# Loading and splitting q and k of the first pair of heads in the stage before the attention

## The reference

```python
qkv = xm @ W_qkv
q, k, v = jnp.split(qkv, 3, axis=-1)          # each (4, 1024, 1024), reshaped to 16 heads of 64
attn = jnp.einsum('bqhd,bkhd->bhqk', q, k) * 64 ** (-0.5)
attn = jax.nn.softmax(attn, axis=-1)
out = jnp.einsum('bhqk,bkhd->bqhd', attn, v).reshape(4, 1024, 1024)
x = x + g_msa * (out @ W_out + b_out)
```

## Time and profile before

| what | value |
|---|---|
| median of 3 runs | 3242.78 us (3240.78 to 3244.02) |
| the profiled execution | 3242.52 us |
| its span in the trace | 3240.4 us |
| projections, first product to last | 557.5 to 1106.4 us |
| attention, first scores to last product with v | 1121.3 to 2274.7 us |
| PE busy | 95% of the span |
| DVE busy | 59% |
| ACT busy | 39% |
| POOL busy | 27% |

### The profile page before, as it was taken

How to read it: one execution, slowest core, us unless ns; L and a number is a source line. 1 busy time by engine, 2 the same in 40 slices (tenths; PEclk the granted TensorE clock), 3 DMA queues, 4 the chain that set the end, 5 groups by cost and what they waited for, 6 DMA issues and landing times. The chain is left out here.

```text
span 3240.4 us, 61734 instructions
## 1 busy us (share of the span) xinstructions
PE 3084.6 (95%) x24696; PEld 2441.5 (75%) x24696; DVE 1904.3 (59%) x2802; ACT 1250.9 (39%) x2370; POOL 863.8 (27%) x578
## 2 busy tenths in 40 slices
PE   8969996999999799999999999999896999999999
PEld 5968885888888677777777777777685888888887
DVE  4369996111221288888888888888564333343332
ACT  2123332222222177777777777777002111111111
POOL 1012222100000044354445434446454111111110
PEclk9989998999999899999999999999997999999999
DMA  4543322333333433323333333332563001000100
GB/s 139 181 181 129 102 72 90 104 106 105 100 104 110 114 99 90 99 80 93 94 92 86 87 104 82 87 93 80 207 237 121 1 27 32 26 32 26 33 14 14
DMA packets 196387, 297.25 MB, mean 92 GB/s; under 512 B 27937, under 2 KB 105761, under 8 KB 194103
## 3 DMA queue, kind: packets, MB, share of 16 engines
q1 hardware_dynamic: 182576, 276.54, 27.4%
q0 software_dynamic: 4288, 14.68, 1.3%
q10 hardware_dynamic: 9296, 2.77, 0.4%
HBM read 190.44 MB, written 103.49 MB: 91 GB/s over the span
## 5 line engine op out<-in xcount | busy, mean ns | idle before, releaser
L1267 DVE TENSOR_REDUCE b_nm<-b_ps 128x1 f32<-128x1024 f32 x512 | 601.9, 1217 | 16.3 <-PE b_ps L1208 3.2
L1174 ACT ACTIVATE b_p<-b_ps,b_nm 128x1024 f32<-128x1024 f32 x512 | 565.0, 1113 | 41.2 <-DVE b_nm L1267 41.2
L1237 PE MATMUL b_po<-b_pt,b_v 128*64 128x256 f32 x4096 | 498.3, 385 | 0.8 <-DVE b_pt L1287 0.8
L1179 ACT ACTIVATE b_pt<-b_tp_act 128x512 f32<-128x512 f32 x512 | 308.7, 603 | 304.9 <-PE b_tp_dve L1220 304.9
L1287 DVE COPY b_pt<-b_tp_dve 128x512 f32<-128x512 f32 x512 | 351.5, 686 | 116.9 <-PE b_tp_dve L1220 116.8
L1220 PEld LDWEIGHTS b_tp_act<-ident,b_p 64*128 64x128 f32 x4096 | 312.1, 138 | 129.4 <-issue 100.6
L1237 PEld LDWEIGHTS b_po<-b_pt,b_v 128*64 128x64 f32 x4096 | 271.8, 136 | 128.7 <-ACT b_pt L1179 0.9
L1220 PE MATMUL b_tp_act<-ident,b_p 64*128 64x64 f32 x4096 | 347.7, 225 | 2.4 <-issue 2.4
L1220 PE MATMUL b_tp_dve<-ident,b_p 64*128 64x64 f32 x4096 | 347.5, 225 | 0.0
L1629 ACT ACTIVATE d_ge<-d_pf,d_b 128x512 f32<-128x512 f32 x128 | 88.1, 689 | 598.6 <-PE d_pf L1651 598.6
L1718 DVE CAST d_gh<-d_ge 128x512 fp32r<-128x512 f32 x128 | 68.7, 537 | 421.5 <-ACT d_ge L1629 421.5
(11 more groups left out here) (228 smaller groups left out, 5771.3 us busy)
## 6 DMA issues: line engine op xcount, KB each, us to landing
b_raw_q<-q_t SPq DMA_DIRECT2D x128, 256.0 KB, 4.4
q_t<-p_qk SPq DMA_DIRECT2D x64, 256.0 KB, 2.0
k_t<-p_qk SPq DMA_DIRECT2D x64, 256.0 KB, 2.0
v_n<-p_vs SPq DMA_DIRECT2D x32, 512.0 KB, 3.2
b_raw_k<-k_t SPq DMA_DIRECT2D x128, 128.0 KB, 4.4
b_v<-v_n SPq DMA_DIRECT2D x32, 512.0 KB, 3.9
b_rb<-inv SPq DMA_DIRECT2D x64, 256.0 KB, 3.8
o_t<-b_ot SPq DMA_DIRECT2D x32, 512.0 KB, 2.6
```

The costliest lines, as they stand in the source:

```text
L1174: act.activation(pr[k % 4][:], ps[k % 2][:], ACT.Exp, bias=nm[:, k % 4:k % 4 + 1], accum_out=rs[:, n:n + 1]).then_inc(exp_done, 1)
L1179: act.activation(dst, src, ACT.Copy).then_inc(t_out[0], 1)
L1237: mm = pe.matmul(po[rows, (blk % 2) * 2 * P:(blk % 2 + 1) * 2 * P], vt[u][:, kc, rows], pt[blk % 2][h][:, kc, :], start=(kc == 0), stop=(k ...
L1267: dve.tensor_reduce(nm[:, k % 4:k % 4 + 1], ps[k % 2][:], axis=AX.X, op=ALU.max, negate=True).then_inc(max_done, 1)
```

## The change

`program` now allocates eight tiles, `pair0` (the halves of q and k for the two heads of pair 0), before `projections` and on the right side of SBUF, and frees them after `attention`. In the last group of `projections` SP issues the eight loads of pair 0 ahead of the group's first store, into raw tiles of that stage. `q_t[0]` and `k_t[0]` were written in groups 0 and 1. DVE waits for all eight loads and makes the eight split operations ahead of the copies of v. In `attention` set 0 of the halves is `pair0`. The eight first loads, the eight split operations, the waits on `first_split` in PE and POOL and three semaphores are gone. `projections` has two semaphores more.

```diff
@@ -739,7 +739,7 @@
     dve.tensor_scalar(var_eps[:], mean_var[:, :, 1], EPS, None, ALU.add).then_inc(var_ready, 1)
 
 
-def projections(nc, t, ident, mod_t, y, q_t, k_t, v_n, wqk):
+def projections(nc, t, ident, mod_t, y, q_t, k_t, v_n, pair0, wqk):
 
 
 
@@ -764,6 +764,8 @@
         xl = ring(ctx, nc, "p_xl", 2, [P, KC, 512], F32R)
         qk = ring(ctx, nc, "p_qk", 4, [P, 512], F32)
         vs = ring(ctx, nc, "p_vs", 2, [P, INNER], F32)
+        raw_q = ring(ctx, nc, "p_raw_q", 2, [P, S], F32)
+        raw_k = ring(ctx, nc, "p_raw_k", 2, [P, S // 2], F32)
         pt = banks(ctx, nc, "p_pt", 2)
         pm = banks(ctx, nc, "p_pm", 4)
         (w_split, ln_step, half_set, var_ready, rstd_ready, z_done, t_done, xm_done, rounded, x_split,
@@ -771,6 +773,7 @@
             ctx, nc, "proj", "w_split ln_step half_set var_ready rstd_ready z_done t_done xm_done rounded x_split mb_done "
             "m_done qk_done v_done w_rounded qk_free v_free", first=True)
         w_in, ones_set = sems(ctx, nc, "proj", "w_in ones_set")
+        pair_in, pair_rounded = sems(ctx, nc, "proj", "pair_in pair_rounded")
         first_in = sems(ctx, nc, "proj", " ".join("first_in%d" % i for i in range(GT)))
         y_in = sems(ctx, nc, "proj", "y_in0 y_in1")
         qk_out = sems(ctx, nc, "proj", " ".join("qk_out%d" % i for i in range(4)))
@@ -800,9 +803,19 @@
             sp.sem_inc(qk_free, 4)
             sp.sem_inc(v_free, 2)
 
+            def load_pair0():
+                for h in range(2):
+                    for half in range(2):
+                        rows = slice(half * D1, (half + 1) * D1)
+                        sp.dma_start(raw_q[h][rows, :], q_t[0, h * D1:(h + 1) * D1, :]).then_inc(pair_in, 16)
+                        sp.dma_start(raw_k[h][rows, :], k_t[0, h * D1:(h + 1) * D1, half * S // 2:(half + 1) * S // 2]
+                                     ).then_inc(pair_in, 16)
+
             def turn(b, last):
                 for hf in range(2):
                     g = b * 2 + hf
+                    if last and hf:
+                        load_pair0()
                     for n in range(NQK):
                         dst = q_t if n < PAIRS else k_t
                         sp.wait_ge(qk_done, g * NQK + n + 1)
@@ -975,6 +988,14 @@
                         norm(g + 1, b + hf, 1 - hf)
                         normed(g + 1, 1 - hf, 0)
                         normed(g + 1, 1 - hf, 1)
+                    if not more:
+                        dve.wait_ge(pair_in, 128)
+                        for h in range(2):
+                            dve.tensor_copy(pair0["qh"][h][:], raw_q[h][:])
+                            dve.tensor_copy(pair0["kh"][h][:], raw_k[h][:]).then_inc(pair_rounded, 1)
+                            dve.wait_ge(pair_rounded, h + 1)
+                            dve.tensor_tensor(pair0["ql"][h][:], raw_q[h][:], pair0["qh"][h][:], ALU.subtract)
+                            dve.tensor_tensor(pair0["kl"][h][:], raw_k[h][:], pair0["kh"][h][:], ALU.subtract)
                     for m in range(NV):
                         n = m // 2
                         if more and m % 2 == 0:
@@ -987,7 +1008,7 @@
             turn(B - 1, True)
 
 
-def attention(nc, t, ident, q_t, k_t, v_n, inv, o_t, wo, wo_raw, o_first, o_first_raw):
+def attention(nc, t, ident, q_t, k_t, v_n, pair0, inv, o_t, wo, wo_raw, o_first, o_first_raw):
 
 
 
@@ -1015,10 +1036,10 @@
             return ctx.enter_context(nc.sbuf_tensor("b_" + name, shape, dt))
         raw_q = ring(ctx, nc, "b_raw_q", 2, [P, S], F32)
         raw_k = ring(ctx, nc, "b_raw_k", 2, [P, SK], F32)
-        qh = [ring(ctx, nc, f"b_qh{u}", 2, [P, S], F32R) for u in range(2)]
-        ql = [ring(ctx, nc, f"b_ql{u}", 2, [P, S], F32R) for u in range(2)]
-        kh = [ring(ctx, nc, f"b_kh{u}", 2, [P, SK], F32R) for u in range(2)]
-        kl = [ring(ctx, nc, f"b_kl{u}", 2, [P, SK], F32R) for u in range(2)]
+        qh = [pair0["qh"], ring(ctx, nc, "b_qh", 2, [P, S], F32R)]
+        ql = [pair0["ql"], ring(ctx, nc, "b_ql", 2, [P, S], F32R)]
+        kh = [pair0["kh"], ring(ctx, nc, "b_kh", 2, [P, SK], F32R)]
+        kl = [pair0["kl"], ring(ctx, nc, "b_kl", 2, [P, SK], F32R)]
         vt = ring(ctx, nc, "b_v", 2, [P, BT, P], F32)
         pr = ring(ctx, nc, "b_p", 4, [P, S], F32)
         pt = [ring(ctx, nc, f"b_pt{u}", 2, [P, BT, 2 * P], F32) for u in range(2)]
@@ -1032,13 +1053,12 @@
         tp_dve = banks(ctx, nc, "b_tp_dve", 2)
         po, = banks(ctx, nc, "b_po", 1)
         (q_in, ones_set, raw_used, rounded, qk_ready, s_done, max_done, exp_done, inv_done, inv_turned, inv_stored, rb_in,
-         t_done, av_done, o_out, o_scaled, o_stored, o_free, first_split, ri_clear) = sems(
+         t_done, av_done, o_out, o_scaled, o_stored, o_free, ri_clear) = sems(
             ctx, nc, "attn", "q_in ones_set raw_used rounded qk_ready s_done max_done exp_done inv_done inv_turned inv_stored rb_in "
-            "t_done av_done o_out o_scaled o_stored o_free first_split ri_clear", first=True)
+            "t_done av_done o_out o_scaled o_stored o_free ri_clear", first=True)
         t_out = sems(ctx, nc, "attn", "t_out0 t_out1")
         t_begun, = sems(ctx, nc, "attn", "t_begun")
         wo_in, next_rounded, next_split, o_first_in = sems(ctx, nc, "attn", "wo_in next_rounded next_split o_first_in")
-        first_in = sems(ctx, nc, "attn", "first_in0 first_in1")
         v_in = sems(ctx, nc, "attn", "v_in0 v_in1")
         block = ctx.enter_context(nc.Block())
 
@@ -1060,11 +1080,6 @@
                              ).then_inc(v_in[u], 16)
 
             def first_load():
-                for h in range(2):
-                    for half in range(2):
-                        sp.dma_start(raw_q[h][HALF[half], :], q_t[0, HALF[h], :]).then_inc(first_in[h], 16)
-                        sp.dma_start(raw_k[h][HALF[half], :], k_t[0, HALF[h], half * SK:(half + 1) * SK]
-                                     ).then_inc(first_in[h], 16)
                 sp.dma_start(vt[0][:], v_n[0].rearrange("(c k) d -> k c d", k=P)).then_inc(v_in[0], 16)
 
             def spread(p, u):
@@ -1132,7 +1147,6 @@
                 pool.wait_ge(rb_in, 32 * p + 32)
                 pool.tensor_tensor(ot[u][:], ot[u][:], rb[u][:], ALU.mult).then_inc(o_scaled, 1)
 
-            pool.wait_ge(first_split, 4)
             pool.sem_inc(raw_used, 1)
             split(1, 0, 1)
             with pool.Fori(0, LAST2) as i:
@@ -1197,9 +1211,7 @@
                 g, u, s = i * TS + k, (k // STEPS) % 2, k % STEPS
                 h = (s // 2) % 2
                 q0 = (s // QB) * 2 * P + (s % 2) * P
-                if k in (0, 2):
-                    pe.wait_ge(first_split, k + 2)
-                elif s == 0:
+                if k and s == 0:
                     pe.wait_ge(qk_ready, i * TURN + k // STEPS)
                 if k >= 2:
                     pe.wait_ge(exp_done, g - 1)
@@ -1302,13 +1314,6 @@
             dve.memset(ri[:], 0.0).then_inc(ri_clear, 1)
             dve.wait_ge(ri_clear, 1)
 
-            for h in range(2):
-                dve.wait_ge(first_in[h], 64)
-                dve.tensor_copy(qh[0][h][:], raw_q[h][:])
-                dve.tensor_copy(kh[0][h][:], raw_k[h][:]).then_inc(first_split, 1)
-                dve.wait_ge(first_split, 2 * h + 1)
-                dve.tensor_tensor(ql[0][h][:], raw_q[h][:], qh[0][h][:], ALU.subtract)
-                dve.tensor_tensor(kl[0][h][:], raw_k[h][:], kh[0][h][:], ALU.subtract).then_inc(first_split, 1)
             maximum(0, 0)
             maximum(1, 1)
             for k in range(0, TS, 2):
@@ -1800,14 +1805,18 @@
             raw, rest = over_raw(part, nc, name, shape)
             return (high, rest), raw
 
+        first_pair = ExitStack()
         with ExitStack() as part:
             wqk, wqk_raw = split_pair(part, "w_qk", [P, KC, 2 * INNER])
             graph_attention(nc, t, ident, gp, cg, pn, y, wqk, wqk_raw)
-            projections(nc, t, ident, mod_t, y, q_t, k_t, v_n, wqk)
+            pair0 = {name: [first_pair.enter_context(nc.sbuf_tensor(f"pair0_{name}{h}", [P, cols], F32R, side="right"))
+                            for h in range(2)] for name, cols in (("qh", S), ("ql", S), ("kh", S // 2), ("kl", S // 2))}
+            projections(nc, t, ident, mod_t, y, q_t, k_t, v_n, pair0, wqk)
         with ExitStack() as part:
             wo, wo_raw = split_pair(part, "w_out", [P, INNER // P, F])
             o_first, o_first_raw = split_pair(part, "o_first", [P, INNER // P, 512])
-            attention(nc, t, ident, q_t, k_t, v_n, inv, o_t, wo, wo_raw, o_first, o_first_raw)
+            attention(nc, t, ident, q_t, k_t, v_n, pair0, inv, o_t, wo, wo_raw, o_first, o_first_raw)
+            first_pair.close()
             w1_raw, w1l = over_raw(ctx, nc, "w1", [P, KC, MLP], top=True)
             output_projection(nc, t, gates, o_t, y, y2, wo, o_first, w1_raw)
         mlp(nc, t, ident, mod_t, gates, y2, out, w1_raw, w1l)
```

## The result

The changed kernel took 3230.58 us in the median of 7 runs (3228.53 to 3233.67), the kernel before 3240.78 us in 7 runs of the same comparison (3237.7 to 3244.02). The ratio is 0.9969, 95% interval 0.9959 to 0.9978: faster by 0.31%. The profiled execution took 3231.34 us, its span is 3229.2 us. Repeated in another comparison the change gave 3229.17 against 3239.79 us, ratio 0.9969 (0.9957 to 0.9980).

The account below looks back on a forecast made before the run. PE was taken as the bound, busy 3084.6 of 3240.4 us. The earlier first maximum gave 10.46 us, clock and added work 0, so 3242.8 - 10.5 = 3232.3 us; range 3230.4 to 3234.9, carried to 3229.3 to 3236.8.

Parts of the forecast that it names:

- PE's start: Attention's start: PE's first score matmul 0.47 us behind SyncE's first issue, at 1112.42 us of the trace.
- Rival (a): Attention's entry: PE isn't ready, above all lacking instructions; time 3235.5 to 3238.7 us; chance 0.09.
- rows 9: Profile rows on instruction queues before the change: q8 moved one block between 1085 and 1095, none between 1095 and 1135.
- The first maximum: Attention's start: DVE's first row maximum 1.69 us behind PE's start, at 1114.11 against 1124.57, 10.46 us earlier.
- the drain of the projections: Projections to attention: 5.58 us in which the old stage drains, which the change does not touch.
- The clock: Attention's start: PE's granted clock still 0.50, back within 4 to 9 us; worth -1 to +1.5 us, taken as 0.
- The added part: Projections' last group: eight loads more on SyncE and eight operations (5.9 us) on DVE, both costing nothing.
- The covers: Projections' last group: DVE's idle 46.9 us hides the splits; the ring of four banks hides SyncE's loads.
- The slip of ACT's copy: Projections' last group: ACT's fifth copy, due at 1053.2, may slip by 2 us waiting for the first q store.
- Rival (c): Projections' last group: late loads block DVE's v copies; PE waits past 1088.6, each us costing one; 3249.3 or more; chance 0.03.
- Pair 1: Attention: loads of pair 1 begin 12 us earlier, POOL's split moves to about 1122.6 to 1136, PE never waits.
- Rival (b): Attention: a later release, pair 1's split or pair 0's v, takes the gain back; 3237.6 to 3242.8 us; chance 0.07.

Follow-up runs that it names:

- run with the loads alone: Changed kernel with pair 0's loads kept in the projections' last group but both heads' splits back at the attention's start; 3232.45 us, ratio 0.9975.
- half stores: Changed kernel with the projections' last store of v cut in two, the first half issued once copied; 3227.37 and 3228.86 us in two comparisons.
- six splits: Changed kernel with pair 0's split in the projections' last group made six times instead of once; 3229.36 us, ratio 0.9961.
- nine splits: Changed kernel with pair 0's split in the projections' last group made nine times instead of once; 3238.54 us, ratio 0.9995.
- run with both edits: Changed kernel with the last store of v in two halves and 12 unread matmuls behind PE's last projection product; 3227.24 us, ratio 0.9958.
- seven idle matmuls: Changed kernel with the last v store halved, 12 unread matmuls ending the projections and seven more behind the second score tile; 3226.03 us, ratio 0.9955.
- run with 16 idle matmuls: Changed kernel with 16 matmuls, results never read, behind PE's last product of the projections; 3226.83 us, ratio 0.9963.

## Why the prediction was right

**PE's start.** Predicted 0.47 us behind SyncE's first issue, by the next stage's row; it was 0.35, and 0.34 or 0.35 in every run in which it had its data. Rival (a), something else that PE lacks at entry, is ruled out for this kernel. As rows 9 had it, PE's instructions were there: in the trace after, q8 moved one block between 1085 and 1095 and none from 1095 to 1125. The fetch that the Trainium skill, "Runtime: NRT & Kernel Launch", section Instruction fetch mechanics, warns of behind a taken branch whose target isn't in the loaded window cost nothing that this trace shows.

**The first maximum.** Predicted 10.46 us earlier, measured 10.35. Its pace of 1.69 us was read from the third tile (1127.17 to 1128.86), which the prediction calls the second; as a pace at the low clock it served all the same. The small parts nearly cancel: PE 0.12 us quicker at entry, the maximum 0.07 slower behind PE, and the drain of the projections 5.74 instead of 5.58 us. That last part was costed at nothing. The semaphores of the stage are cleared in seven steps where there had been six, which fits the 0.16 us, though no run tests it alone. Before and in the changed kernel:

```profile
L65 POOLq EVENT_SEMAPHORE_RANGE_CLEAR  x6: 45/46/131, 1110.7 to 1111.5; - x6
...
L65 POOLq EVENT_SEMAPHORE_RANGE_CLEAR  x7: 45/45/131, 1111.3 to 1112.2; - x7
```

The run with the loads alone shows the two halves of the sum: 6.5 us for the loads, 3.9 for the splits, of which 1.1 is the maximum behind head 1's split.

**The clock.** Predicted at 0.50 at PE's start and worth 0 between -1 and +1.5. It was 0.50, as PE still stood for 6.09 us, and back after 8.59 us instead of 9.12:

```profile
1113.01:1121.60 8.59, 6.71 (x40) 4.77 (x40) 5.00 (x6) 2.89 (x5) 0.00 (x0) 0.50 0.92 228
1121.60:1130.00 8.40, 6.52 (x92) 4.70 (x94) 6.62 (x8) 6.28 (x13) 6.16 (x4) 1.00 0.35 82
```

The third exponential moved by 10.26 us and the 33rd by 10.31, so the clock gave and took nothing. The reason given, that the pattern of work was kept, is weaker than it looked, and that the term came out at 0 is in part luck. The half stores show that one pattern can raise it after 3.5 or after 12.3 us, and in the five profiles in which PE's start and the first maximum lie as in the changed kernel it was back after 8.1 to 12.9 us. The latest of them, with six splits, has its 33rd exponential 0.92 us later; that lies within the bound of 1 us that the prediction set for it.

**The added part.** The covers held as reckoned: loads landed at 1053.3 (predicted 1053.0), splits ended by 1059. The slip of ACT's copy was 0.11 us where up to 2 were allowed, because the first store landed sooner than the estimate of 1055. Rival (c) had its turning point right: PE waits once DVE is busy beyond the first copy's last date. That every us then costs one left out the clock: with nine splits a wait of 8.68 us made the group 10.30 us longer.

**Pair 1.** POOL's split ran from 1123.76 to 1136.9 (predicted 1122.6 to 1136), 11.0 us earlier than before instead of 12, and PE never waited for it. Rival (b) is ruled out.

**The total.** 3232.3 predicted, 3230.58 measured. The size of the gain was right (10.5 predicted, 10.2 by the medians); the kernel before measured 3240.78 in the longer comparison instead of the 3242.78 from which the sum started, so most of the 1.7 us between forecast and time is its starting point. The two profiled executions differ by 11.2 us, of which 10.35 lie at the boundary. From the first maximum to the end of the span the trace before has 2115.8 us and the two of the changed kernel 2114.4 and 2113.7. Of these 1.4 and 2.1 us, 1.1 and 1.5 lie behind the first matmul of the output projection (953.45 us to the end of the span before, 952.38 and 951.96 in the changed kernel), in stages whose instructions are the same. What makes them up stays open.

## What to carry to other kernels

Where stages meet at a barrier, read the wait of the bounding engine at the first operation of the next stage and divide it into the drain, the load and the preparation. Data that was finished long ago can be loaded and prepared in the stage before, in the idle time of its engines, and then only the drain is left. Check three covers when doing so: the idle time of the engine that prepares, the queue that the loads are put into, and the ring behind that queue; and expect the operations queued behind the removed ones (here the first maximum) to count too.

## What the hardware showed that was not expected

The time until PE's clock was back after a boundary differed for one and the same kernel: 3.5 us and 12.3 us behind PE's start with the half stores. At this boundary it moves the third exponential by 1.2 us (12.60 to 13.79) and the 33rd by 1.9 us (79.24 to 81.10), a part of the scatter between runs. The fall before it varied too: in the ten profiles without idle matmuls it came 3.6 to 5.3 us after the end of PE's last product.

The clock also fell from 1.00 to 0.50 while PE was at work: in the run with both edits at 1115.1, 5.5 us after PE's start, though since then PE had waited at most 1.94 us at a time, and in the run with only the loads moved 6.3 us after PE's start, with one wait of 2.34 us. With seven idle matmuls in that pause it did not fall in the profiled run. But the pause alone can't be the cause: the run with 16 idle matmuls has the same waits, 2.35 us at the barrier (2.39 in the run with both edits) and 1.94 us behind the second tile, and its clock stayed at 1.00. The cause stays open.
